# Last experts of a two-layer decoder: the weighted sum of two expert rows per token made by adding transfers into the output in DRAM

## The reference, cut to what matters

```
prob      = softmax(x @ gate_w.T)              # 12 experts
top2      = the two largest, weights p1/(p1+p2), p2/(p1+p2)
position  = rank of the (slot, token) pair among the pairs of its expert
kept      = position <= CAP                    # CAP = ceil(2048 / 12 * 1.25) = 214
y[e]      = (silu(x_e @ w1[e].T) * (x_e @ w3[e].T)) @ w2[e].T
out[tok]  = xa[tok] + sum over its kept pairs of weight * y[expert][position]
```

## Time and profile before

| what | us |
| --- | --- |
| median of 3 runs (3706.37 to 3713.87) | 3709.27 |
| the profiled execution's own time | 3703.98 |
| its span | 3702.1 |
| its last section: first DVE instruction | 3560.63 |
| first row gather is issued | 3584.03 |
| first copy of an expert's output begins | 3601.41 |
| last copy of an expert's output begins | 3647.33 |
| first gather of rows back | 3650.77 |
| last addition to `xa` begins | 3698.41 |

### The profile page before, as it was taken

The page is one execution under the profiler, slowest core; times in us unless marked ns, Lnnn a source line. Parts: engine busy times, 40 slices in busy tenths (PEclk is TensorE's granted clock), DMA queues, the critical chain, the costliest instruction groups (busy, mean ns, idle before and its releaser), DMA issues. The chain is left out here.

```text
span 3702.1 us, 34730 instructions
## 1 busy us (share of the span) xinstructions
PE 3217.6 (87%) x11033; PEld 1578.1 (43%) x11045; DVE 2427.2 (66%) x4472; ACT 1770.6 (48%) x3342; POOL 1205.7 (33%) x963
## 2 busy tenths in 40 slices
PE   3750699999999799999999999799999888898854
PEld 3330344444444355555555555344444444444332
DVE  8769899999999555555555555534322367888654
ACT  4748566666665334343433334343311136777621
POOL 0423699999997010010000000023485020000014
PEclk9975799999999899999999999999999997999977
DMA  7124425352432222212111111345421120000046
GB/s 255 47 63 167 145 93 147 96 149 91 141 98 74 93 74 64 83 64 74 60 55 58 57 57 43 126 142 175 171 105 54 40 80 1 1 1 1 1 154 216
DMA packets 201318, 334.67 MB, mean 90 GB/s; under 512 B 25648, under 2 KB 76208, under 8 KB 198064
## 3 DMA queue, kind: packets, MB, share of 16 engines
q1 hardware_dynamic: 187904, 298.69, 24.5%
q0 software_dynamic: 12208, 33.57, 3.2%
q10 hardware_dynamic: 1024, 0.20, 0.0%
HBM read 217.69 MB, written 114.69 MB: 90 GB/s over the span
## 5 line engine op out<-in xcount | busy, mean ns | idle before, releaser
L1282 POOL TENSOR_TENSOR sc_dBu<-sc_dtu,xa 128x1024 f32<-128x1024 f32 x256 | 540.6, 2136 | 38.4 <-DMA sc_dtu<-scan_dtu 29.5
L1192 PE MATMUL y_ps<-sc_g,ident 128*128 128x512 f32 x1024 | 475.9, 600 | 18.2 <-POOL sc_g L1270 11.8
L1306 DVE TENSOR_TENSOR_SCAN sc_dA<-sc_dA,sc_dBu 128x1024 f32<-128x1024 f32 x160 | 365.1, 2282 | 6.8 <-POOL sc_dBu L1282 6.8
L1565 ACT ACTIVATE c_p<-c_ps,c_sm 128x512 f32<-128x512 f32 x256 | 195.7, 774 | 354.5 <-DVE c_sm L1606 354.5
L1605 DVE TENSOR_REDUCE c_sm<-c_ps 128x4 f32<-128x2048 f32 x64 | 146.7, 2292 | 313.2 <-PE c_ps L1528 313.2
L1246 ACT ACTIVATE sc_dA<-sc_dt,a_neg 128x511 f32<-128x511 f32 x512 | 329.6, 676 | 11.1 <-DVE sc_g L1306 9.8
L1192 PEld LDWEIGHTS y_ps<-sc_g,ident 128*128 128x128 f32 x1024 | 190.0, 190 | 255.7 <-issue 169.4
L1598 DVE SCALAR_TENSOR_TENSOR xa<-c_ps,c_sm,xa 128x512 f32<-128x512 f32 x256 | 192.2, 751 | 146.9 <-PE c_ps L1518 133.2
L1518 PE MATMUL c_ps<-c_wo,c_oT 128*128 128x512 f32 x512 | 246.5, 605 | 2.3 <-DVE xa L1598 1.6
L1499 PE MATMUL c_ps<-u,c_wq 128*128 128x512 f32 x512 | 233.0, 598 | 4.5 <-DMA c_wq<-in_c_wq_dram 4.5
L1547 PE MATMUL c_ps<-c_pT,c_v 128*128 128x512 f32 x512 | 230.8, 593 | 1.6 <-DVE c_pT L1617 1.6
(11 more groups left out here) (516 smaller groups left out, 6089.6 us busy)
## 6 DMA issues: line engine op xcount, KB each, us to landing
kv_w<-in_c_wkv_dram SPq DMA_DIRECT2D x32, 512.0 KB, 4.1
cross_keys<-kv_out SPq DMA_DIRECT2D x64, 256.0 KB, 2.0
cross_values<-kv_out SPq DMA_DIRECT2D x128, 128.0 KB, 1.9
c_kT<-cross_keys SPq DMA_DIRECT2D x64, 256.0 KB
c_rk<-cross_rk SPq DMA_DIRECT2D x64, 256.0 KB
c_v<-cross_values SPq DMA_DIRECT2D x64, 256.0 KB, 2.7
expert_rows<-e_yt SPq DMA_DIRECT2D x63, 256.0 KB, 2.0
xa<-scan_bc SPq DMA_DIRECT2D x48, 256.0 KB, 8.8
```

Of the source, the lines that this page charges most:

```text
L1192: ins = pe.matmul(yps[:, k % 2, :], ident[:], g[:, c % GS, n, :], start=False, stop=(m == NCH - 1 and n == NG - 1))
L1282: pool.tensor_tensor(dBu[:, c % 3], spread(dtu[:, k % DT, :], NG), bc[:, m * NG:(m + 1) * NG, :], ALU.mult).then_inc(s_dBu, 1)
L1306: dve.tensor_tensor_scan(to.rearrange("p n s -> p (n s)"), dA[:, c % 2].rearrange("p n s -> p (n s)"), dBu[:, c % 3].rearrange("p n s -> p ...
L1565: ins = act.activation(pr[:, j, :], ps[:, SB + j, :], ACT.Exp, scale=rq[:, j:j + 1], bias=bias[:, j:j + 1], accum_out=l[:, j:j + 1])
```

## The change

Stages 3 and 4 are replaced. SP stores all 16 tiles of `xa` to `out` at the start of the section. PE and DVE bring each pair's weight into the order of the places: the weight is split into three bf16 pieces, multiplied into the one-hot matrix of the tiles (`part`), and 32 more products `low.T @ part` give `wl`, one weight for each place. The copies from PSUM to `yt` multiply by `wl`. POOL then adds each tile `yt` to the rows of `out` in DRAM that the list `to` names, by an indirect transfer with `compute_op=ALU.add`. The adding transfers of one expert start only when those of the expert before it have landed (`s_sum`), since a token's two rows come from two experts.

Places that no pair takes, and tokens of the last two token tiles, get a row of the last two token tiles as their target, one of their own for each place of a tile (`spill`). Those two token tiles therefore hold something else when the adding is over. The tiles `yt` are still stored to `parts`, and at the end POOL gathers the rows of these two token tiles (4 gathers), DVE adds them to `xa` with weights 0 or 1, and SP stores the two tiles again.

The `yt` ring grows from 4 to 8, and a copy into it waits for the adding transfer as well as for the store. The row gathers and the adding transfers share POOL's list.

```diff
-XR1, YR1 = 6, 4
+XR1, YR1 = 6, 8
+LAST_TWO = NTT - 2
...
+        wls = ps[:, 6, 0:3 * TL]
...
             def _(sp):
+                for j in range(NTT):
+                    sp.dma_start(tiles[:, j, :], xa[:, j, :]).then_inc(s_out, 16)
                 for t in range(TL):
                     sp.wait_ge(s_ya if t % 2 else s_yd, t // 2 + 1)
                     sp.dma_start(parts[t * HALF:(t + 1) * HALF, :], yt[:, t % YR1, :]).then_inc(s_st[t % YR1], 16)
-                for j in range(NTT):
-                    sp.wait_ge(s_cmb, SLOTS * (j + 1))
-                    sp.dma_start(out[:, j, :], xa[:, j, :]).then_inc(s_out, 16)
-                sp.wait_ge(s_out, 16 * NTT)
+                sp.wait_ge(s_sum, 32 * NE1)
+                for i in range(2):
+                    sp.wait_ge(s_cmb, SLOTS * (i + 1))
+                    sp.dma_start(tiles[:, LAST_TWO + i, :], xa[:, LAST_TWO + i, :]).then_inc(s_out, 16)
+                sp.wait_ge(s_out, 16 * (NTT + 2))
...
                 pool.wait_ge(s_ids, 1)
-                for t in range(TL):
+
+                def taken(t):
                     if t >= XR1:
                         pool.wait_ge(s_xT, t - XR1 + 1)
                     pool.indirect_dma_start(xs[:, t % XR1, :], None, rows,
                                             bass.IndirectOffsetOnAxis(ap=ids[:, t:t + 1], axis=0)
                                             ).then_inc(s_x[t % XR1], 16)
+
+                def given(t):
+                    pool.wait_ge(s_ya if t % 2 else s_yd, t // 2 + 1)
+                    pool.indirect_dma_start(tokens, bass.IndirectOffsetOnAxis(ap=to[:, t:t + 1], axis=0),
+                                            yt[:, t % YR1, :], None, compute_op=ALU.add).then_inc(s_sum, 16)
+
+                for t in range(XR1):
+                    taken(t)
+                pool.wait_ge(s_out, 16 * NTT)
+                for e in range(NE1):
+                    for t in range(2 * e + XR1, 2 * e + XR1 + 2):
+                        if t < TL:
+                            taken(t)
+                    if e:
+                        pool.wait_ge(s_sum, 32 * e)
+                    for t in (2 * e, 2 * e + 1):
+                        given(t)
                 pool.wait_ge(s_row, 1)
                 for q in range(YR1):
                     pool.wait_ge(s_st[q], 16 * len(range(q, TL, YR1)))
-                for n in range(NA):
-                    j, k = divmod(n, SLOTS)
-                    if n >= GR:
-                        pool.wait_ge(s_cmb, n - GR + 1)
-                    a = k * NTT + j
-                    pool.indirect_dma_start(gy[:, n % GR, :], None, parts,
-                                            bass.IndirectOffsetOnAxis(ap=row_u[:, a:a + 1], axis=0)
-                                            ).then_inc(s_g[n % GR], 16)
+                for i in range(2):
+                    for k in range(SLOTS):
+                        pool.indirect_dma_start(gy[:, k, i, :], None, parts,
+                                                bass.IndirectOffsetOnAxis(ap=own_u[:, k, i:i + 1], axis=0)
+                                                ).then_inc(s_get, 16)
+                pool.wait_ge(s_sum, 32 * NE1)
...
+                def weighed():
+                    pe.wait_ge(s_part, 1)
+                    for a in range(NA):
+                        ins = pe.matmul(wls, low[:, a, :], part[:, a].rearrange("p k i -> p (k i)"), start=(a == 0),
+                                        stop=(a == NA - 1))
+                    ins.then_inc(s_wls, 1)
+
                 turned(0)
+                weighed()
...
                         if t >= YR1:
+                            act.wait_ge(s_sum, 32 * ((t - YR1) // 2 + 1))
                             act.wait_ge(s_st[t % YR1], 16 * (t // YR1))
-                        act.activation(yt[:, t % YR1, :], ps[:, 6, :], ACT.Copy).then_inc(s_ya, 1)
+                        if e == 1:
+                            act.wait_ge(s_wl, 1)
+                        act.activation(yt[:, t % YR1, :], ps[:, 6, :], ACT.Copy, scale=wl[:, t:t + 1]).then_inc(s_ya, 1)
...
                 turned(0)
+                dve.wait_ge(s_wls, 1)
+                dve.tensor_reduce(wl[:], wls.rearrange("p (k i) -> p i k", k=3), AX_X, ALU.add).then_inc(s_wl, 1)
+                dve.wait_ge(s_wl, 1)
...
-                        dve.tensor_copy(yt[:, t % YR1, :], ps[:, 5, :]).then_inc(s_yd, 1)
-                for n in range(NA):
-                    j, k = divmod(n, SLOTS)
-                    dve.wait_ge(s_g[n % GR], 16 * (n // GR + 1))
-                    if k:
-                        dve.wait_ge(s_cmb, n)
-                    dve.scalar_tensor_tensor(out=xa[:, j, :], in0=gy[:, n % GR, :], scalar=w[:, k, j:j + 1],
-                                             in1=xa[:, j, :], op0=ALU.mult, op1=ALU.add).then_inc(s_cmb, 1)
+                        dve.tensor_scalar(yt[:, t % YR1, :], ps[:, 5, :], wl[:, t:t + 1], None, ALU.mult).then_inc(s_yd, 1)
+                dve.wait_ge(s_out, 16 * NTT)
+                dve.wait_ge(s_get, 16 * SLOTS * 2)
+                for i in range(2):
+                    for k in range(SLOTS):
+                        if k:
+                            dve.wait_ge(s_cmb, i * SLOTS + k)
+                        x = xa[:, LAST_TWO + i, :]
+                        dve.scalar_tensor_tensor(out=x, in0=gy[:, k, i, :], scalar=own_w[:, k, i:i + 1], in1=x,
+                                                 op0=ALU.mult, op1=ALU.add).then_inc(s_cmb, 1)
```

More of the change, by code:

```diff
@@ L2754, in _ @@
                 own.after(dve.tensor_tensor(pos[:], pos[:], M[:], ALU.mult))
-                rank, over, half, first, hi, lo, row, expert = (dst[:, i] for i in range(8))
+                rank, over, half, first, hi, lo, expert = (dst[:, i] for i in range(7))
                 own.after(dve.tensor_reduce(rank.rearrange("p k j -> p (k j)"), pos[:], AX_X, ALU.add))
@@ new lines, in _ @@
+                dve.tensor_tensor(to[:], spill[:], number[:], ALU.add)
+                whole = w[:].rearrange("p k j -> p (k j)")
+                own.after(dve.tensor_copy(pieces[:, 0], whole))
+                own.after(dve.tensor_tensor(rest[:, 0], whole, pieces[:, 0], ALU.subtract))
+                own.after(dve.tensor_copy(pieces[:, 1], rest[:, 0]))
+                own.after(dve.tensor_tensor(rest[:, 1], rest[:, 0], pieces[:, 1], ALU.subtract))
+                own.after(dve.tensor_copy(pieces[:, 2], rest[:, 1]))
@@ L2782, in turned @@
+                for i in range(3):
+                    ins = dve.tensor_tensor(part[:, :, i, :], pairs[:], along(pieces[:, i], TL), ALU.mult)
+                ins.then_inc(s_part, 1)
                 def turned(e):
@@ L2857, in program @@
             cross1(nc, A, xa, d, spare, ident, kn, vn, kst, wqc)
[L2858 removed]
+        experts1(nc, A, rows, parts, xa, out, ident, ctx)
 def _laid_out(inputs):
```

59 lines of the change are left out of this document (39 added, 20 removed).

## The result

| | before | changed |
| --- | --- | --- |
| median, us (20 runs each, same chip) | 3706.78 | 3713.64 |
| lowest to highest | 3698.91 to 3714.28 | 3702.69 to 3719.64 |
| profiled execution: own time, span | 3703.98, 3702.1 | 3712.68, 3710.6 |

The ratio of the changed kernel to the one before is **1.002**, with a 95% interval of 1.0012 to 1.0029. That is 7 us, on the edge of what can be told from no change, and on the slower side. The time lies inside the wide range of 3690 to 3738, but outside the forecast's own 3696 to 3703, and the interval leaves out the forecast of 3701.

The account below looks back on a forecast made before the run. PE was taken to fill the expert loop, with a 54.9 us tail on POOL and DMA behind it. Span 3604.0 + 11 x 6.7 + 16.0 = 3693.7, 8.4 below 3702.1, gave median 3701; range 3690 to 3738, forecast's own 3696 to 3703.

Parts of the forecast that it names:

- T: Expert loop: the period from one expert's pair of adding transfers to the next, taken as 6.7 us on average.
- g(0): Front of the loop: start of the first adding transfer, taken as 3604.0.
- g(11): End of the loop: start of the last expert's adding pair, g(0) + 11T, with 16.0 us behind it to the end.
- T = 1.25 (issue of the first of the two): POOL's list in the loop: the first adding transfer's issue takes 1.25 us of each period.
- slow adding: Rival, DMA engines in the loop: an adding transfer keeps them for s = 3.6, T = 10.2, median 3739; slower side, chance 0.25.
- the wait of 0.55 for the rest of the first transfer: Adding pair: the second transfer waits for the first's remaining engine time, 1.8 - 1.25 = 0.55 us, counted in L.
- s: DMA engines: the time one adding transfer keeps them, taken as 1.8 us with twice a gather's reading.
- costs no more than a gather: Rival, adding transfers: T falls to 6.1, and to 5.15 for the last three experts; median 3691, chance 0.13.
- Read, then write: Rival, adding transfers: old rows must arrive before the write starts, T = 7.15, median 3706; chance with its surroundings 0.28.
- T at least 6.1: Feed bound in the loop: row gathers behind adding transfers, then PE's path, need 12.25 us for two experts.
- PE's clock falls: Rival, PE in the loop: 2 us gaps lower its clock, feed bound T = 8.1, median 3716, chance 0.06.
- L + 1.55: Sign in POOL's timeline: spacing of adding pairs, L being an adding transfer's time from issue to landing, 5.05 us.

Follow-up runs that it names:

- plain_scatter: Changed kernel with plain indirect writes in place of the adding transfers, so the sum is left out; ratio to the kernel before 0.9982.
- ring12: Changed kernel with the ring of gathered row tiles at 12 instead of 6; ratio to the kernel before 1.0013.
- filled_clock: Changed kernel with ten unread extra products on PE ahead of the turning of experts 4, 6, 8 and 10; ratio to the kernel before 1.0003.
- drop_stores: dropped_rows with the 24 stores of output tiles to `parts` put back, though nobody reads them; ratio to the kernel before 1.0006.
- dropped_rows: Changed kernel with row-tile ring 12, pairless places dropped, last two token tiles added like the others, their stores and gathers removed; ratio to the kernel before 0.9987.
- dropped_again: The same kernel as dropped_rows, measured a second time in another group; ratio to the kernel before 1.001.
- the first group: Four variants of the changed kernel measured on one chip: row-tile ring of 12, plain writes, second target tensor, dropped rows; ratios 1.0013, 0.9982, 0.9923, 0.9987.
- drop_ring8: dropped_rows with the ring of gathered row tiles at 8 instead of 12; ratio to the kernel before 0.9983.

## Why the prediction was wrong, step by step

The prediction's sum was 3604.0 + 11T + 16.0 with T = 6.7. Set against the profiled execution:

| term | predicted | measured | difference |
| --- | --- | --- | --- |
| first adding transfer, g(0) | 3604.0 | 3599.1 | -4.9 |
| 11 periods, if only landings set them | 73.7 | 82.5 | +8.8 |
| more, from the four periods that wait for PE (10.1) and the one of 8.41 (0.9) | 0 | 11.0 | +11.0 |
| from g(11) to the end | 16.0 | 18.0 | +2.0 |
| span | 3693.7 | 3710.6 | +16.9 |

**The step that failed first: "T = 1.25 (issue of the first of the two)".** The 1.25 is the gather's 0.95 of the earlier trace rows with 0.30 behind it, carried over to a transfer that adds. It is 1.88 here. The prediction named this as one of its conditions ("if POOL's issue of an adding transfer is clearly over 0.95"), but gave it no range and no price. The rival "slow adding" named it too ("POOL may also need longer to write out two reads for each row"), again without a price. Put into the prediction's own formula, with the rest kept: the landing is 3.6 + 0.63 + 0.9 = 5.1, the wait of 0.55 for the rest of the first transfer disappears, since 1.88 is already longer than 1.8, and T = 1.88 + 5.1 + 0.3 = 7.3. Measured is 7.5. So this one row, taken from the wrong kind of transfer, accounts for most of the 8.8. plain_scatter shows the 0.99 beside the 1.58.

**Nearly right: the size of the service.** s was taken as 1.8, from a gather's 0.89 doubled; for 128 rows 2.14 alone and 1.99 beside stores were measured. The formula makes too much of it: with s = 2.14 it would give T = 7.9, and ring12 has 7.37 and 7.59 there. The rule of the Trainium skill that a reduce runs at half a copy's rate (Collectives: The Full Stack, the bandwidth ceiling) gives the direction, but not the size here: 2.14 is 2.4 times a gather's 0.89, and 1.99 is 2.9 times the 0.68 of a plain indirect write (these two beside stores). The measurement decides. "Slow adding" with s = 3.6 and "costs no more than a gather" both fall. "Read, then write", T = 7.15, comes close in size, and no run tells whether its mechanism has a part: the issue explains the landing without it.

**The step that failed second: "T at least 6.1", the feed bound "below 6.7".** The mechanism was right and each term too small. For two experts the prediction had 12.25, and the chain shows 17.87:
- the adding pair 3.79 instead of 2.5: +1.3, the issue again;
- the row gather's landing 6.10 instead of 1.25 + 3.6: +1.25. It was priced as if the queue were empty, while two adding transfers of about 2 each stand ahead of it;
- PE and the copy, with 0.17 between, 7.2 instead of 4.6: +2.6. About 2.3 of it is the clock (the turning 2.13 instead of 1.09, `hidden` 3.29 instead of 1.99 in PE's timeline);
- from the copied output to POOL's issue 0.79 instead of 0.3: +0.5.

**Wrong: the clock at 1.00.** "PE's clock falls" had a chance of 0.06. It is the part of the result that filled_clock shows alone: 8.2 of 11.0 us. The rival's own argument against it, that slower products fill the gaps, didn't hold: behind a gap of 6.09 the turning ran at 2.13, the lower level. But the clock fell only in part, to 0.80 on the mean: the gaps come as one of 4.5 to 6.2 for every two experts and not as 2 for each, and the later products between two gaps run at full clock. So a time near this rival's (3713.6 against 3716) is partly luck. Its T = 8.1 everywhere isn't what happened: the average of 8.5 is made of six periods around 7.5, set by landings, and five of 9.7 on average.

**The front** came 4.9 earlier than predicted. 1.8 of it is the first row gather, at 3582.24 instead of 3584.03, outside the part that changed. About 1.5 is the added products: they were priced at 2.1 and cost 0.6. They stand in the chain with 1.92, but the turning behind them took 1.13 for 8 blocks, at the upper level of the clock, where it had 0.29 for one, about 2.3 for eight, before. `hidden(0)` ends 10.9 behind the first row gather, before it was 10.3. The remaining 1.6 is that the gap of 4.15 on ACT, which g(0) = 3604.0 took as likely, isn't there in this execution.

**The smaller signs.** The DMA share in the loop is 0.82, over the 0.8 named. PE's four gaps together are 22.5 for eight experts, 2.8 for each and not 2, and it waits for `e_xs` as named. The spacing is L + 1.55 only with the issue corrected to L + 2.2, and in seven of eleven periods.

**The end** is 2.0 longer: 1.2 by the two issues of 1.88 (3.7 instead of 2.5), and 0.7 by a landing of 4.33 instead of 3.6. The 2.9 from the last addition to the end is 2.98.

The direction hung on little: the sum gave itself a margin of 0.76 in T (6.7 against the 7.46 of no change), and every term of T but the wake of 0.3 came from a transfer of another kind. The bounds were put around L and s, but the issue time that stands in T twice was taken as known.

## What to carry to other kernels

A chain of transfers that each wait for the one before to land is priced by latency: issue of the first, issue and landing of the second, wake. Here that was 7.5 us per pair with the engines half idle, and neither a longer ring nor shorter lists nor dropped rows brought it below 7.3 on average. Giving alternate links another target took 32.5 us of waiting away at once, though what it leaves to be joined isn't priced. When a step moves under a busy loop, cost the loop's feed with the new neighbours in its queue, and PE's part at the clock that its gaps will leave it. And give the issue of an instruction that isn't in the trace bounds of its own, as much as its landing. Where rows are dropped, divide the engines' time by the bytes that moved, not by the transfers.

## What was not expected of the hardware

**The issue of an adding transfer** costs POOL 1.58 against 0.95 to 0.99 for a gather or a plain write of the same 128 rows, and still 1.45 with 96 rows. Rows with a target past the bound are dropped: the queue moves 107 rows instead of 128 for each transfer, at no lower issue time (1.56). The engines' work is 2.14 for 128 rows added, against 0.68 for 128 rows written.

**A standstill that moves.** In seven of the twelve variants (drop_stores and all runs listed below it in the table) the front is 21.7 to 25.0 instead of 15.7 to 18.6. ACT's first step of the loop starts 3.8 to 8.2 behind the end of `hidden(0)`, the products that it reads, where it is 0 to 0.8 in the others, and PE and DVE show gaps of up to 4.8 in the same stretch. The releasers that the trace names are long past by then. This is that step, the same kernel in dropped_rows and in dropped_again:

```profile
3588.10 0.38 ACT L2736 ACTIVATE e_bs<-e_ps 64x256 f32<-64x256 f32 x1 [33.00 <-PE e_ps L2698]
```

```profile
3604.55 0.38 ACT L2736 ACTIVATE e_bs<-e_ps 64x256 f32<-64x256 f32 x1 [41.02 <-PE e_lps L2698]
```

From the first row gather (3577.0 and 3585.4) these are 11.1 and 19.1. The text of the kernel is the same, so it belongs to the execution or the chip. The chips differ: none of the four variants of the first group shows it, three of them with a ring of 12, and on the other three chips all seven with a ring of 8 or 12 do. The delay grows with the number of gathers issued back to back: 3.8 to 3.9 with a ring of 8, 7.6 to 8.2 with a ring of 12. In two of these traces that were read for it, the step comes at about the time when the traffic of these gathers ends (3604.55 and about 3606 in dropped_again, 3596.94 and 3597.5 in drop_ring8). Whether the gathers cause it wasn't tried, and neither the changed kernel nor filled_clock, both with a ring of 6, shows it. This is up to 0.2% of the time, as much as the differences between the variants here: a reason to compare their loops as well as their ratios. The gap of 4.15 of the kernel before looks like the same thing, one step later, which isn't shown either.
